# Weight copy ahead of the context copy, two TensorE products exchanged, row maxima begun at slot 10, first stacks in halves

## What is computed

```
h   = einsum(concat(pos, nest[nesting(ids)], seg[segments(ids)]), W)      # token embedding
x   = layernorm(h); q, k, v = split(x @ qkv_w.T + qkv_b)                   # 8 heads of 16
h   = h + (softmax(q k^T / 4) v) @ out_w.T + out_b
x   = layernorm(h)
w   = relu(softmax(x @ gate_w.T) - sigmoid(x @ thr_w.T) / 4), normalised   # 4 experts
out = h + sum_e w_e * (relu(x @ fc1_e.T) @ A_e @ B_e @ fc2_e.T)
```

## Time and profile before

| | before |
|---|---|
| median of three runs | 1198.49 us |
| the profiled execution | 1197.47 us |
| its span in the trace | 1195.7 us |
| PE busy | 1052.9 us, 88% |
| DVE busy | 952.5 us, 80% |
| ACT busy | 821.4 us, 69% |
| POOL busy | 681.9 us, 57% |

### The profile page before, as it was taken

One profiled execution on the slowest core, in us unless ns is written; L12 is line 12 of the kernel. 1 busy time (PEld: TensorE's weight loads), 2 busy tenths in 40 slices (PEclk: granted clock), 3 DMA queues, 4 the chain that ended last, 5 costly groups with the idle time before them and its releaser, 6 DMA issues.

```text
span 1195.7 us, 20256 instructions
## 1 busy us (share of the span) xinstructions
PE 1052.9 (88%) x6158; PEld 393.8 (33%) x6158; DVE 952.5 (80%) x2442; ACT 821.4 (69%) x1578; POOL 681.9 (57%) x684
## 2 busy tenths in 40 slices
PE   5268889999999999999999999999999999999965
PEld 2012233333333333333333333333333333333322
DVE  7399888888888888888888888888888888888322
ACT  2216777777777777777777777777777777776841
POOL 1844575676556665665566665765556656632231
PEclk8558999999999999999999999999999999999986
DMA  2544545554544445555544455545544455541111
GB/s 73 136 100 107 126 105 129 125 121 118 126 120 112 112 119 135 119 121 121 128 114 112 115 122 133 118 120 123 127 109 113 116 130 122 121 98 39 55 56 36
DMA packets 93242, 132.43 MB, mean 111 GB/s; under 512 B 18109, under 2 KB 69822, under 8 KB 86918
## 3 DMA queue, kind: packets, MB, share of 16 engines
q1 hardware_dynamic: 91584, 129.54, 45.1%
q10 hardware_dynamic: 1550, 1.59, 0.5%
HBM read 89.20 MB, written 35.01 MB: 104 GB/s over the span
## 4 chain that ended last, share of the span: by engine, by line
PE 53%; DVE 25%; issue 9%; ACT 8%; DMA 3%; POOL 1%; SPq 0%; POOLq 0%; ACTq 0%; DVEq 0%
PE pv L723 13%; PE mix L733 13%; DVE negmax L1009 10%; PE sc L710 9%; PE mix L787 7%; ACT probs L578 4%; PE mix L770 3%; PE mix L808 3%; PE mix L792 3%; DVE bn L999 2%; DVE qk L994 2%; ACT hid L632 2%; DVE out_sb L1088 2%; DVE h_sb L986 2%; DVE h L1034 2%
## 5 line engine op out<-in xcount | busy, mean ns | idle before, releaser
L1009 DVE TENSOR_REDUCE negmax<-mix 128x1 f32<-128x512 f32 x1024 | 671.9, 680 | 122.7 <-PE mix L733 119.6
L578 ACT ACTIVATE probs<-sc 128x512 f32<-128x512 f32 x1024 | 574.3, 596 | 218.2 <-PE sc L710 214.1
L733 PE MATMUL mix<-kstk,qstk 96*128 96x512 bf16 x1024 | 360.2, 395 | 84.0 <-ACT turned L622 22.4
L710 PE MATMUL sc<-qstk,kstk 120*128 120x512 bf16 x1024 | 361.7, 381 | 1.5 <-ACT probs L578 1.2
L723 PE MATMUL pv<-probs,vals 128*32 128x512 f32 x2048 | 273.8, 601 | 0.0
L733 PEld LDWEIGHTS mix<-kstk,qstk 96*128 96x128 bf16 x1024 | 92.3, 98 | 434.7 <-DVE negmax L1009 179.1
L514 POOL TENSOR_TENSOR ctxh<-ctx_sb,rdenb 128x512 f32<-128x512 f32 x64 | 81.2, 1270 | 221.0 <-DMA rdenb<-rden_dram 220.6
L787 PE MATMUL mix<-xn2T,fc1T_sb 128*128 128x512 f32 x256 | 135.4, 612 | 8.0 <-DVE negmax L1009 8.0
L710 PEld LDWEIGHTS sc<-qstk,kstk 120*128 120x128 bf16 x1024 | 99.7, 98 | 103.7 <-issue 29.8
L494 POOL TENSOR_TENSOR qk<-qk,rstdb 128x512 f32<-128x512 f32 x64 | 81.3, 1272 | 92.0 <-DMA rstdb<-rstd_dram 92.0
L632 ACT ACTIVATE hid<-mix 128x512 f32<-128x512 f32 x128 | 76.1, 596 | 35.4 <-PE mix L787 35.4
(11 more groups left out here) (141 smaller groups left out, 1067.4 us busy)
## 6 DMA issues: line engine op xcount, KB each, us to landing
stack_dram<-pieces SPq DMA_DIRECT2D x192, 128.0 KB
rdenb<-rden_dram SPq DMA_DIRECT2D x64, 256.0 KB
qstk<-stack_dram SPq DMA_DIRECT2D x32, 384.0 KB, 6.6
kstk<-stack_dram SPq DMA_DIRECT2D x32, 384.0 KB, 8.7
rstdb<-rstd_dram SPq DMA_DIRECT2D x32, 256.0 KB, 3.4
qstk<-stack_dram SPq DMA_DIRECT2D x32, 256.0 KB, 7.0
kstk<-stack_dram SPq DMA_DIRECT2D x32, 256.0 KB, 9.2
wrow<-w_dram SPq DMA_DIRECT2D x32, 256.0 KB
```

Source lines behind the costliest of these rows:

```text
L578: act.activation(probs[:, c % 8, i % 2], sc[:, i % RING], ACT.Exp).then_inc(s_exp, 1)
L710: pe.matmul(sc[:, i % RING, :], kstk[0:KROWS, u, h, j * P:(j + 1) * P], qstk[0:KROWS, u, h, :], start=True, stop=True).then_inc(s_score, 1)
L733: pe.matmul(max_bank(m), qstk[0:STK, u, h, j * P:(j + 1) * P], kstk[0:STK, u, h, :], start=True, stop=True).then_inc(s_mxmm, 1)
L1009: dve.tensor_reduce(negmax[:, m // NT, m % NT:m % NT + 1], max_bank(m), AX.X, ALU.max, negate=True).then_inc(s_max, 1)
```

## The change

Five edits. `MSTART` goes from 8 to 10: the maxima of a sequence, and `cut_max`, come two slots later. `embed` and `fc1_3` exchange their slots (1 and 2), with `relu` of `fc1_3` and DVE's work on the embedding moved to suit. ACT copies `wT` right behind `rT`, before `mT` and before the context, and the context copy goes behind one exponential; the wait for the bank of `mT` then names the copy of `mT` (the last of the three). The stacks of sequence 0 are loaded in two halves of the heads, and PE waits for each half alone. Two setup pieces move by a slot.

```
-MSTART = 8
+MSTART = 10
 PRODUCTS = [
-    ("project", -2), ("embed", 4), ("fc1_3", -3), ("low", -3), ...
+    ("project", -2), ("fc1_3", -3), ("embed", 4), ("low", -3), ...
 ACT_WORK = [
-    (1, 2, "qk", 3, 0), (2, 2, "relu", -3, 3), (3, 1, "qk", 3, 1), ...
+    (1, 1, "relu", -3, 3), (1, 2, "qk", 3, 0), (3, 1, "qk", 3, 1), ...
-    (12, 0, "rT", 4, 0), (12, 0, "mT", 1, 0), (12, 0, "ctx", 0, 0), (12, 1, "wT", -2, 0), (13, 1, "relu", -2, 2),
+    (12, 0, "rT", 4, 0), (12, 0, "wT", -2, 0), (12, 0, "mT", 1, 0), (12, 1, "ctx", 0, 0), (13, 1, "relu", -2, 2),
 DVE_WORK = [
-    (2, 1, "add_pos", 4, 0), (3, 0, "stats1", 4, 0), (3, 1, "stats1", 4, 1), (4, 0, "weigh", -3, 0),
-    (5, 0, "moments1", 4, 0), (6, 1, "finish", -3, 0), (7, 1, "invert_den", -1, 0),
+    (3, 0, "add_pos", 4, 0), (4, 0, "weigh", -3, 0), (4, 1, "stats1", 4, 0), (5, 0, "stats1", 4, 1),
+    (6, 0, "moments1", 4, 0), (6, 1, "finish", -3, 0), (7, 1, "invert_den", -1, 0),
...
+            def load_half_heads(g):
+                heads = slice(4 * g, 4 * g + 4)
+                for side in range(2):
+                    sp.wait_ge(s_pcout[side], 48)
+                    for row, p, n in STACK:
+                        dst, src = ((qstk, stack_dram[0, 0, :, p, heads].unsqueeze(1).broadcast_to([HC, n, 4, S])),
+                                    (kstk, stack_dram[0, 1, :, 0:n, heads]))[side]
+                        sp.dma_start(dst[row:row + n * HC, 0, heads, :], src).then_inc(s_half[g][side], 16)
...
-                "stack": lambda b, u, side: (load_qstack, load_kstack)[side](b, u),
+                "stack": lambda b, u, side: (load_qstack, load_kstack)[side](b, u) if b else load_half_heads(side),
...
-                if m == 0:
+                if m == 0 or b == 0 and m == 16:
                     for side in range(2):
-                        upto(pe, s_stk[side], b, 48)
+                        if b == 0:
+                            pe.wait_ge(s_half[m // 16][side], 48)
+                        else:
+                            upto(pe, s_stk[side], b, 48, 0)
...
-                    if name == "mT" and runs(t - 2):
-                        return t - 2, (s_wT, 1, 1)
                     if name == "mT" and not runs(t + 1):
-                        return t + 4, (s_rT, 1, 1)
+                        return (t - 2, (s_wT, 1, 1)) if t > 0 else (t + 4, (s_rT, 1, 1))
```

More of the change, by code:

```diff
@@ L54 @@
 PRODUCTS = [
-    ("project", -2), ("embed", 4), ("fc1_3", -3), ("low", -3), ("none", None), ("xn2T", -2), ("out", -3), ("gates", -2),
+    ("project", -2), ("fc1_3", -3), ("embed", 4), ("low", -3), ("none", None), ("xn2T", -2), ("out", -3), ("gates", -2),
     ("turn_gates", -2), ("fc1_0", -2), ("fc1_1", -2), ("mT", 1), ("q", 4), ("fc1_2", -2), ("k", 4), ("v", 4),
@@ L62 @@
 ACT_WORK = [
-    (1, 2, "qk", 3, 0), (2, 2, "relu", -3, 3), (3, 1, "qk", 3, 1), (4, 0, "ctx", -1, 1), (5, 2, "xn2T", -2, 0),
+    (1, 1, "relu", -3, 3), (1, 2, "qk", 3, 0), (3, 1, "qk", 3, 1), (4, 0, "ctx", -1, 1), (5, 2, "xn2T", -2, 0),
     (8, 0, "gates", -2, 0), (9, 0, "gate_exp", -2, 0), (9, 1, "relu", -2, 0), (10, 1, "relu", -2, 1),
-    (12, 0, "rT", 4, 0), (12, 0, "mT", 1, 0), (12, 0, "ctx", 0, 0), (12, 1, "wT", -2, 0), (13, 1, "relu", -2, 2),
+    (12, 0, "rT", 4, 0), (12, 0, "wT", -2, 0), (12, 0, "mT", 1, 0), (12, 1, "ctx", 0, 0), (13, 1, "relu", -2, 2),
     (15, 2, "v", 4, 0),
@@ L265, in tower @@
         s_stk = [sem(f"s_stk{a}") for a in "qk"]
+        s_half = [[sem(f"s_half{g}{a}") for a in "qk"] for g in range(2)]
         s_mxmm, s_max = sem("s_mxmm"), sem("s_max")
@@ L333, in store_piece @@
                 if p == 0:
-                    upto(sp, s_stk[side], b - 2, 48)
+                    if b == 2:
+                        sp.wait_ge(s_half[1][side], 48)
+                    upto(sp, s_stk[side], b - 2, 48, 0)
                 sp.dma_start(stack_dram[b % 2, side, :, p].rearrange("c h s -> h c s"),
                              pieces[:, side, p, :]).then_inc(s_pcout[side], 16)
+            def load_half_heads(g):
[6 more added lines that the diff above has]
+                        sp.dma_start(dst[row:row + n * HC, 0, heads, :], src).then_inc(s_half[g][side], 16)
             def load_qstack(b, u):
@@ L877, in step @@
                 for c in range(SLOTS):
-                    if t == -4 and c == 2:
+                    if t == -4 and c == 3:
                         fold_positions()
@@ L1115, in step @@
                         copy_weights()
-                    if t == -4 and c == 6:
+                    if t == -4 and c == 7:
                         cut_folded()
```

## The result

The changed kernel took 1141.27 us (median of 4 runs, 1139.75 to 1142.55) against 1197.93 (4 runs): ratio 0.953, 95% interval 0.9509 to 0.955. The forecast was 1153, its range ended at 1146. The sign and the size of a step were right; 11.7 us of gain were not foreseen.

What follows compares the result with a forecast made beforehand. PE was taken to set the pace, each stall worth its length. Gains of 14.3, 26.9 and 6.4 against losses of 1.3 and 0.9 gave 45.4 us off 1197.47, so 1152.1, or 1153 by the median; range 1146 to 1168.

Steps and rivals of the forecast that it cites:

- 4.0 + 2.4 - 0.9: Start and end: 4.0 us from half stacks, 2.4 from four fewer maxima before the first score, 0.9 lost in step 30.
- Slot 10: `MSTART` 10: 28 x 0.51 us at `fc1_0`, 2.4 less at the start, 0.9 more at the end; 15.8 alone.
- The exchange: Embedding and `fc1_3` swapped: the `h_sb` stall moves by a slot, 0.05 us longer, 26 times, a loss of 1.3.
- The copies: ACT's `wT` copy ahead of `mT` and context: PE's 0.96 us wait in slot 12 goes 28 times, 26.9 us.
- The halves: First stacks loaded in halves: first maxima tile 4.0 us earlier, near 50.7; rival that they bring nothing, chance 0.10.
- `fc1_0` stall: PE waits at `fc1_0` for the first maximum, behind `cut_max`; slot 10 removes 0.51 us in each of 28 steps.
- `wT` stall: PE's second maxima tile of slot 12 waits for ACT's copy of `wT`; all 0.96 us goes, 28 times.
- moved `h_sb` stall: PE's wait for DVE's `h_sb` moves to slot 3, 0.05 us longer; 0.7 to 0.8 in the profile's brackets.
- `qk` wait: PE's maxima tiles wait for DVE's `qk`, 0.5 us in the step read; claimed to stay as it was.
- margins of 0.04 to 0.06: Slack before PE needs `mT`'s bank: 0.04 us behind DVE's maxima, 0.01 to 0.06 behind ACT's copies; claimed enough.
- rival of late maxima: `max_in` lands after a step's first score is due, each microsecond over 5.8 paid 28 times; ends slower, chance 0.05.
- rival in which `add_pos` comes before the maximum: On DVE in the exchange: the 0.84 us `h_sb` stall would go 26 times, 22 us, giving 1130; chance 0.06.

Runs made afterwards that it cites:

- x_both: Changed kernel with DVE's `add_pos` one piece earlier, ahead of the maximum it stood behind, and k's add one piece earlier: 1111.94 us (0.9283).
- x_pool: Changed kernel with `add_pos` and k's add each one piece earlier, and POOL's `rstd1` behind the second half of the gated products: 1107.38 us (0.925).

## Why the prediction was wrong

**The step that failed** is the one from the list of waits to the sum: I read each stall's worth as "28 times", from steps 2 to 29, at the length it has in a full step, and gave the filling and the end only 4.0 + 2.4 - 0.9. The edits act there as well. Slot 10 gave 19.1 alone, not 15.8: 2.9 in steps 0 to 2 instead of 0.5, because `cut_max` is slow there in steps 0 and 2 and in steps 0 and 1 the stall stands at another line, and 4.45 up to the first score instead of 2.4, because `cut_max` is slow there too and the four maxima gave about 3. The exchange, entered as a loss of 1.3, pays: in the profiled runs 2.6 before the first score, 0.6 in steps 0 to 2, 0.7 over steps 3 to 27, -0.7 in 28 to 30 and 0.7 behind, 3.9 in all (5.1 by the medians), with the doubt about the first 2.6 said above. The copies give 28.1 to 28.4, not 26.9, 1.4 of it behind step 30 when they stand alone. There the kernel before has a wait of DVE for the softmax sums from DRAM, 2.50 us at 1156.37; with the copies alone it is 0.66, and with the exchange alone or in the changed kernel it is gone.

**The halves**: 5.3 us earlier at the first maximum instead of 4.0. Some of it is SP's queue, which issues the first transfer at 42.81 instead of 43.38. That is not the halves' doing, since with whole stacks in the changed kernel it is 42.81 as well; there the first maximum comes at 54.35, so the halves themselves give 4.9. What I had too small is that I carried over how long the full queue took (7.9 us for k's 128 KB): with half the bytes queued, k's 64 KB landed 3.3 us after their issue.

The Trainium skill's estimate ("DMA: Bandwidth & Descriptors", "Anatomy of one DMA"), near 49, was closer to the 49.45 than my 50.7. It was so by luck: with the queue's real start, 0.57 earlier, mine would be 50.1 and the other estimate 48.4. The Trainium skill gives that fit for transfers issued from GpSimd, and these are SP's. The Trainium skill's advice against small transfers did not decide here. Of the 5.5 us that the halves bring at the first score of the changed kernel 3.2 are left in the profiled runs; steps 0 to 2 take 0.8 back and steps 28 to 30 take 1.7. The 1.7 is a wait that the kernel with whole stacks does not have: in step 28 of the changed one DVE waits for the softmax sums from DRAM, and PE for the maximum behind it, so that this step lasts 31.97 us instead of 30.05. On DVE and PE:

```profile
994.63 0.35 DVE L1042 RECIPROCAL rden<-den 128x32 f32<-128x32 f32 x1 [2.10 <-DMA den<-den_dram]
...
995.58 0.39 PE L749 MATMUL mix<-kstk,qstk 96*128 96x512 bf16 x1 [1.38 <-DVE negmax L1023]
```

**Right**: the `fc1_0` stall (0.51), the `wT` stall (0.96), the moved `h_sb` stall (0.89, in slot 3), the `qk` wait as before, a step of 32.31 against 32.35. The margins of 0.04 to 0.06 held. The rival of late maxima did not come.

**Right by luck**: the exchange's price in a step. I wrote that POOL waits 1 us longer and has it back before the context comes. True, but in that microsecond it runs beside other work of DVE: 0.84 us a step where `cut_max` stands in slot 8. It is free only because slot 10 moves `cut_max` away, which I had not seen. And the rival in which `add_pos` comes before the maximum is real, as an edit: with k's add moved as well it is `x_both`.

**Open**: what makes two transfers late. The sums from DRAM hold up step 28 in the changed kernel and in `x_both` (32.12 us), and not in `x_pool` (30.05); the broadcast `rstdb` in the filling lands 3.0 to 4.3 us after its issue. Neither was tried by itself, nor what costs the 0.8 us of steps 0 to 2 with the halves.

## What to carry to other kernels

A stall's worth is its length times every step in which its cause runs, not those in which one line of the list of waits names it; go through the first and last steps as closely as through a full one. An engine with much idle time is still not free to be late: what it shares with another engine decides, so see what stands on the neighbour's timeline in the new place. And test edits alone and undone: one that costs 20 us alone was worth 5 in company.

## What the runs showed of the hardware

A DVE cast of 128x32 from SBUF to SBUF takes 0.18 us alone and 1.00 beside a POOL product, ending with it. Maxima read from PSUM were not slower beside POOL: in the kernel before, the 442 that lie beside its work take 0.68 us, as do the 288 that lie beside none. `onehot` is held in the changed kernel as well: 19 of its 32 take over 0.5 us, and each of them ends 0.15 us behind a POOL product. PE waits for it twice, both times in the filling (min/median/max ns, after and before):

```profile
L994 DVE TENSOR_SCALAR onehot<-ids_b,const_sb x32: 340/1123/1447, 19.2 to 944.7; 96x512 bf16<-96x512 bf16 x32
```

```profile
L980 DVE TENSOR_SCALAR onehot<-ids_b,const_sb x32: 336/340/1360, 19.2 to 994.5; 96x512 bf16<-96x512 bf16 x32
```

A 256 KB broadcast from DRAM to SBUF landed 3.0 to 4.3 us after its issue in kernels whose work up to there differs by little.
